# Set-up of a one-core LSTM kernel in another order: load order over two queues, searches before low halves, three PSUM banks for three sums

## The reference

```python
xW = jnp.einsum('ntd,dg->ntg', x, Wx) + b          # x (16, 512, 512), Wx (512, 2048)
def step(carry, xw_t):
    prev_h, prev_c = carry
    a = xw_t + prev_h @ Wh                          # Wh (512, 2048)
    i = jax.nn.sigmoid(a[:, :Hdim])
    f = jax.nn.sigmoid(a[:, Hdim:2 * Hdim])
    o = jax.nn.sigmoid(a[:, 2 * Hdim:3 * Hdim])
    g = jnp.tanh(a[:, 3 * Hdim:])
    next_c = f * prev_c + i * g
    next_h = o * jnp.tanh(next_c)
    return ((next_h, next_c), next_h)
# output: x + all hidden states
```

## Time and profile before

| | us |
|---|---|
| median of 3 runs | 2008.93 (2007.4 to 2013.11) |
| the profiled execution's own time | 2012.29 |
| its span, first to last instruction | 2010.5 |
| VectorE busy in it | 1843.2 |
| TensorE busy in it | 1919.7 |

### The profile page before, as it was taken

The page is one execution under the profiler, slowest core; times in us unless marked ns, Lnnn a source line. Parts: engine busy times, 40 slices in busy tenths (PEclk is TensorE's granted clock), DMA queues, the critical chain, the costliest instruction groups (busy, mean ns, idle before and its releaser), DMA issues.

```text
span 2010.5 us, 144062 instructions
## 1 busy us (share of the span) xinstructions
PE 1919.7 (95%) x65620; PEld 1625.9 (81%) x65620; DVE 1843.2 (92%) x9227; ACT 926.2 (46%) x3217; POOL 2.4 (0%) x13
## 2 busy tenths in 40 slices
PE   0799999999999999999999999999999999999998
PEld 0688888888888888888888888888888888888887
DVE  6899999999999999999999999999999999999998
ACT  2444444444444444444444444444444444444444
POOL 0000000000000000000000000000000000000000
PEclk9999999999999999999999999999999999999999
DMA  4000000000000000000000000000000000000000
GB/s 194 9 20 25 22 14 26 26 21 25 16 19 26 20 26 25 10 25 25 20 25 26 10 25 26 20 26 26 10 25 26 21 25 16 19 26 26 21 15 15
DMA packets 15876, 51.46 MB, mean 26 GB/s; under 512 B 1824, under 2 KB 1824, under 8 KB 14240
## 3 DMA queue, kind: packets, MB, share of 16 engines
q1 hardware_dynamic: 14400, 37.76, 5.3%
q10 hardware_dynamic: 864, 4.49, 0.5%
HBM read 25.46 MB, written 16.78 MB: 21 GB/s over the span
## 4 chain that ended last, share of the span: by engine, by line
PE 72%; DVE 23%; issue 2%; ACT 2%; DMA 1%; SPq 0%; ACTq 0%; DVEq 0%
PE acc L235 34%; PE acc L241 20%; PE acc L247 17%; DVE turned L411 5%; DVE preact L415 4%; DVE products L419 2%; DVE h_halves L442 2%; DVE o_gate L423 2%; DVE h_halves L433 2%; DVE h_feat L437 1%; DVE gates L427 1%; DVE out_ring L465 1%; DMA wx<-in_wx 1%; ACT x_halves L176 1%; DVE w_tops L301 1%
## 5 line engine op out<-in xcount | busy, mean ns | idle before, releaser
L235 PE MATMUL acc<-wx_high,x_halves 128*32 128x256 f16 x16384 | 936.6, 273 | 15.8 <-ACT acc L190 9.3
L235 PE MATMUL acc<-wx_low,x_halves 128*32 128x256 f16 x16384 | 935.8, 273 | 2.7 <-issue 2.4
L241 PE MATMUL acc<-wh_low,h_halves 128*32 128x256 f16 x16384 | 723.5, 274 | 23.9 <-DVE wh_low L315 6.2
L247 PE MATMUL acc<-wh_high,h_halves 128*32 128x256 f16 x16384 | 723.0, 274 | 0.3 <-issue 0.3
L204 ACT ACTIVATE gates<-preact 128x128 f32<-128x128 f32 x1024 | 318.5, 311 | 794.6 <-DVE preact L415 794.6
L411 DVE STREAM_TRANSPOSE turned<-acc 128x256 f32<-128x256 f32 x1024 | 457.1, 446 | 71.0 <-PE acc L247 68.9
L241 PEld LDWEIGHTS acc<-wh_low,h_halves 128*32 128x32 f16 x16384 | 388.2, 96 | 165.3 <-DVE h_halves L433 137.1
L235 PEld LDWEIGHTS acc<-wx_high,x_halves 128*32 128x32 f16 x16384 | 457.7, 97 | 36.8 <-ACT acc L190 11.7
L235 PEld LDWEIGHTS acc<-wx_low,x_halves 128*32 128x32 f16 x16384 | 458.8, 97 | 15.5 <-issue 6.3
L247 PEld LDWEIGHTS acc<-wh_high,h_halves 128*32 128x32 f16 x16384 | 360.9, 96 | 111.8 <-issue 1.1
L190 ACT ACTIVATE acc<-b_rows 128x256 f32<-128x256 f32 x1024 | 345.9, 369 | 0.8 <-issue 0.3
(11 more groups left out here) (57 smaller groups left out, 183.8 us busy)
## 6 DMA issues: line engine op xcount, KB each, us to landing
x_ring<-in_x SPq DMA_DIRECT2D x32, 512.0 KB, 4.3
out<-out_ring SPq DMA_DIRECT2D x64, 256.0 KB, 2.3
wx<-in_wx SPq DMA_DIRECT2D x4, 1024.0 KB, 13.4
wh<-in_wh ACTq DMA_DIRECT2D x4, 1024.0 KB, 17.9
b_rows<-in_b ACTq DMA_DIRECT2D x1, 256.0 KB, 4.5
h_feat<-in_h ACTq DMA_DIRECT2D x1, 32.0 KB, 6.8
```

The lines of the kernel that those rows point to most:

```text
L235: pe.matmul(acc[par][n][32 * j:32 * j + 32, 0:GL], x_halves[:, slot, c], w[:, c, n * Q + j], start=False, stop=False, skip_group_check=True)
L241: pe.matmul(acc[par][n][32 * j:32 * j + 32, 0:GL], h_halves[1 - par][:, c, 0:2], w_low["wh"][:, c, n * Q + j], start=False, stop=False, sk ...
L247: last = pe.matmul(acc[par][n][32 * j:32 * j + 32, 0:GL], h_halves[1 - par][:, c, 1:3], w_high["wh"][:, c, n * Q + j], start=False, stop=c ...
```

## The change

The loop is the same. In the set-up:

- Every chunk of a weight matrix is loaded in two halves of 0.5 MB (4 KB a partition), one on each queue; both halves count on the chunk's semaphore, and the search waits for 32 and not 16. SP's order is Wx halves, x, Wh halves, x; ACT's is Wx halves, h0, Wh halves, bias. Each queue issues 10 DMAs in the set-up, where it issued 6.
- VectorE searches all of Wx, then x, h0 and all of Wh, and only then writes low halves; the bias comes after them.
- ScalarE writes the high halves of x between the high halves of Wh.
- The three sums lie in three PSUM banks (`wx_sums`, `wh_sums`, `x_sums`), and TensorE sums Wx first, then x.

```diff
         @block.sync
         def _(sp):
+            for c in range(C):
+                sp.dma_start(w32["wx"][:, c, 0:Q], wx[:, c, 0:Q]).then_inc(w_loaded["wx"][c], 16)
             sp.dma_start(x_ring[0][:], x[:, 0:CHUNK, :]).then_inc(x_loaded[0], 16)
             for c in range(C):
-                sp.dma_start(w32["wx"][:, c], wx[:, c]).then_inc(w_loaded["wx"][c], 16)
+                sp.dma_start(w32["wh"][:, c, 0:Q], wh[:, c, 0:Q]).then_inc(w_loaded["wh"][c], 16)
...
         @block.scalar
         def _(act):
+            for c in range(C):
+                act.dma_start(w32["wx"][:, c, Q:], wx[:, c, Q:]).then_inc(w_loaded["wx"][c], 16)
+            act.dma_start(h0_feat[:], h0).then_inc(h0_loaded, 16)
+            for c in range(C):
+                act.dma_start(w32["wh"][:, c, Q:], wh[:, c, Q:]).then_inc(w_loaded["wh"][c], 16)
             act.dma_start(b_rows[:], bias).then_inc(b_loaded, 16)
-            act.dma_start(h0_feat[:], h0).then_inc(h0_loaded, 16)
-            for c in range(C):
-                act.dma_start(w32["wh"][:, c], wh[:, c]).then_inc(w_loaded["wh"][c], 16)
...
-            act.wait_ge(wh_scale_ready, 1)
-            for c in range(C):
-                high_of_w("wh", 1, c, wh_high_done)
...
+            act.wait_ge(wh_scale_ready, 1)
+            high_of_w("wh", 1, 0, wh_high_done)
             act.wait_ge(x_loaded[0], 16)
             act.wait_ge(x_scale_ready, 1)
             high_of_x(0, 0)
+            high_of_w("wh", 1, 1, wh_high_done)
             high_of_x(0, 1)
+            high_of_w("wh", 1, 2, wh_high_done)
+            high_of_w("wh", 1, 3, wh_high_done)
...
         @block.tensor
         def _(pe):
             pe.wait_ge(ones_ready, 1)
+            pe.wait_ge(tops_ready, 1)
+            pe.matmul(wx_sums[:, 0:1], ones[:], tops[:, 0:1], start=True, stop=True).then_inc(sums_ready, 1)
             pe.wait_ge(x_top_ready, 1)
...
             for c in range(C):
                 search_w("wx", 0, c)
             dve.wait_ge(dve_setup, count[0])
             dve.tensor_reduce(tops[:, 0:1], w_tops[:, 0], AX.X, ALU.max).then_inc(tops_ready, 1)
-            search_w("wh", 1, 0)
+            dve.wait_ge(x_loaded[0], 16)
+            dve.tensor_reduce(x_top[:], x_ring[0][:], AX.XY, ALU.max, apply_absolute_value=True).then_inc(x_top_ready, 1)
             dve.wait_ge(sums_ready, 1)
...
-            for c in range(1, C):
+            for c in range(C):
                 search_w("wh", 1, c)
-                low_of_w("wx", 0, c - 1, wx_high_done, wx_low_done)
...
-            low_of_x(0, 0)
-            low_of_x(0, 1)
             for c in range(C):
                 low_of_w("wh", 1, c, wh_high_done, wh_low_done)
+                if c < 2:
+                    low_of_x(0, c)
```

More of the change, by code:

```diff
@@ L84, in lstm_kernel @@
         acc = [[psum(f"acc{p}{n}", [128, 512], F32) for n in range(NG)] for p in range(2)]
-        sums = psum("sums", [128, 512], F32)
+        wx_sums = psum("wx_sums", [128, 512], F32)
+        wh_sums = psum("wh_sums", [128, 512], F32)
+        x_sums = psum("x_sums", [128, 512], F32)
         w_loaded = {k: [sem(f"{k}_loaded{c}") for c in range(C)] for k in ("wx", "wh")}
@@ L156, in _ @@
         def _(act):
-            act.dma_start(b_rows[:], bias).then_inc(b_loaded, 16)
+            for c in range(C):
+                act.dma_start(w32["wx"][:, c, Q:], wx[:, c, Q:]).then_inc(w_loaded["wx"][c], 16)
             act.dma_start(h0_feat[:], h0).then_inc(h0_loaded, 16)
             for c in range(C):
-                act.dma_start(w32["wh"][:, c], wh[:, c]).then_inc(w_loaded["wh"][c], 16)
+                act.dma_start(w32["wh"][:, c, Q:], wh[:, c, Q:]).then_inc(w_loaded["wh"][c], 16)
+            act.dma_start(b_rows[:], bias).then_inc(b_loaded, 16)
             def high_of_w(k, n, c, done):
@@ L223, in _ @@
             pe.wait_ge(ones_ready, 1)
+            pe.wait_ge(tops_ready, 1)
+            pe.matmul(wx_sums[:, 0:1], ones[:], tops[:, 0:1], start=True, stop=True).then_inc(sums_ready, 1)
             pe.wait_ge(x_top_ready, 1)
-            pe.matmul(sums[:, 8:9], ones[:], x_top[:], start=True, stop=True).then_inc(x_sum_ready, 1)
-            pe.wait_ge(tops_ready, 1)
-            pe.matmul(sums[:, 0:1], ones[:], tops[:, 0:1], start=True, stop=True).then_inc(sums_ready, 1)
+            pe.matmul(x_sums[:, 0:1], ones[:], x_top[:], start=True, stop=True).then_inc(x_sum_ready, 1)
             pe.wait_ge(tops_ready, 2)
-            pe.matmul(sums[:, 1:3], ones[:], tops[:, 1:3], start=True, stop=True).then_inc(sums_ready, 1)
+            pe.matmul(wh_sums[:, 1:3], ones[:], tops[:, 1:3], start=True, stop=True).then_inc(sums_ready, 1)
             def input_part(slot, par, n):
@@ L328, in _ @@
             dve.tensor_reduce(tops[:, 0:1], w_tops[:, 0], AX.X, ALU.max).then_inc(tops_ready, 1)
-            search_w("wh", 1, 0)
+            dve.wait_ge(x_loaded[0], 16)
+            dve.tensor_reduce(x_top[:], x_ring[0][:], AX.XY, ALU.max, apply_absolute_value=True).then_inc(x_top_ready, 1)
             dve.wait_ge(sums_ready, 1)
-            scale_of(0, 1)
+            scale_of(wx_sums, 0, 1)
             dve.tensor_scalar(half_scale[:, 0:1], wx_scale, 0.5, None, ALU.mult).then_inc(wx_scale_ready, 1)
+            dve.wait_ge(h0_loaded, 16)
+            then(dve.tensor_reduce(tops[:, 2:3], h0_feat[:], AX.XY, ALU.max, apply_absolute_value=True))
             dve.wait_ge(wx_scale_ready, 1)
-            for c in range(1, C):
+            for c in range(C):
                 search_w("wh", 1, c)
-                low_of_w("wx", 0, c - 1, wx_high_done, wx_low_done)
             dve.wait_ge(dve_setup, count[0])
             dve.tensor_reduce(tops[:, 1:2], w_tops[:, 1], AX.X, ALU.max).then_inc(tops_ready, 1)
[L339 to L348, removed]
             def x_bound_of():
-                dve.tensor_scalar(x_bound[:], sums[:, 8:9], TINY, None, ALU.max).then_inc(scale_step, 1)
+                dve.tensor_scalar(x_bound[:], x_sums[:, 0:1], TINY, None, ALU.max).then_inc(scale_step, 1)
             def x_exponent_of():
@@ L376, in _ @@
             x_scale_of()
+            low_of_w("wx", 0, 0, wx_high_done, wx_low_done)
+            dve.wait_ge(sums_ready, 2)
+            scale_of(wh_sums, 1, 3)
+            dve.tensor_scalar(half_scale[:, 1:2], wh_scale, 0.5, None, ALU.mult).then_inc(wh_scale_ready, 1)
+            low_of_w("wx", 0, 1, wx_high_done, wx_low_done)
+            dve.tensor_scalar(top_scale[:], wh_scale, 2.0 ** 13, None, ALU.mult)
+            dve.tensor_scalar(h0_cap[:], wh_scale, h0_scale, None, ALU.mult)
+            dve.tensor_copy(factors[:, 0:1], wx_inverse)
+            dve.tensor_scalar(factors[:, 1:2], wh_inverse, 0.5, None, ALU.mult)
+            dve.tensor_copy(factors[:, 2:3], wh_inverse)
+            then(dve.memset(factors[:, 3:4], 1.0))
             dve.wait_ge(scale_step, 3)
@@ L383, in _ @@
             inverses_of(0)
+            low_of_w("wx", 0, 2, wx_high_done, wx_low_done)
+            low_of_w("wx", 0, 3, wx_high_done, wx_low_done)
+            dve.wait_ge(zeroed, 6)
             dve.wait_ge(x_scale_ready, 1)
@@ L389, in _ @@
                                      ALU.mult, ALU.subtract).then_inc(h_ready, NG)
+            dve.wait_ge(b_loaded, 16)
+            dve.tensor_scalar(b_rows[:, :, 64:GL], b_rows[:, :, 64:GL], 0.5, None, ALU.mult).then_inc(b_ready, 1)
             def low_of_x(chunk, q):
```

11 lines of the change are left out of this document (2 added, 9 removed).

## The result

The changed kernel takes 1995.93 us in the median of 4 runs (1994.72 to 1997.31), the kernel before 2008.45 us (4 runs, 2007.40 to 2013.11). The ratio is 0.9931 with a 95% interval of 0.9918 to 0.9945: faster by 0.7%, or 12.5 us between the medians. The profiled execution took 1997.31 us, with a span of 1995.5 us.

What follows compares the result with a forecast made beforehand. VectorE's work and waits set the first step's start: 64.56 − 20.3 + 5.9 + 3 × 0.18 = 50.7 us. The 13.8 us gain off the 2008.9 us median gives 1995.1 us; 8 in 10 range 1991 to 2002.

Steps and rivals of the forecast that it cites:

- What bounds the kernel: Set-up: VectorE decides when the first step starts; its four waits are 20.3 of 64.56 us, the rest its own work.
- The loads: Set-up loads: stream stays at 424 GB/s; Wx's chunks land at 5.9, 8.4, 10.8 and 13.3 us, Wh's last at 24.6.
- 0.9 us from moving to landing: Set-up loads: time added between a chunk's bytes being moved and its landing; bounds 0.7 to 1.2 us.
- tie at Wh's last chunk: VectorE's fourth Wh search would start at 24.6 us, just when its chunk lands; a later load delays everything one for one.
- Two of the signs: Profile after: no VectorE idle time over 0.3 us after the first search; Wh searches back to back from 18.0 to 26.9.
- holes in the stream: Rival, set-up loads: short transfers leave holes costing 7.2 us; start at 57.9 us, time 2002.3 us; chance 0.08.
- the two queues did not hinder each other: Rival, slower: two queues reading halves of one row hinder each other; at 205 GB/s the time is 2015 us; chance 0.02.
- The walk: VectorE's set-up followed instruction by instruction: Wx searched by 15.6 us, Wh by 26.9, last low halves at 50.8.
- The sum: Set-up: VectorE's work unchanged, only idle time shrinks; first step at 50.7 us, gain 13.8 us.
- Size of transfers: Rule against the forecast, set-up loads: at 341 GB/s the start would move 5.1 us and the time be 2000.2 us.
- The clock: First step at half speed after 4.0 us idle; rivals: clock stays high, 1993.2 us, or rises later, 1997.0; chance 0.08 each.
- x's order: ScalarE in set-up: x's high halves stood behind four chunks of Wh, making VectorE wait 6.2 us; that wait goes.

Runs made afterwards that it cites:

- the versions in which GpSimd stretched VectorE's work: Changed kernel with GpSimd writing low halves of one chunk each of Wx and Wh, or of Wx only: ratio 0.9954 and 0.9922 to the kernel before.

## Why the prediction was right

**What bounds the kernel.** That the start of the first step is all that moves, and that it is VectorE's work plus its idle time, held: 43.25 us of work in 50.92 us. The exceptions are the versions in which GpSimd stretched VectorE's work, and, by 0.2 us, the one with low halves between the searches, in which TensorE's x product ended last.

**The loads.** Chunks every 2.47 us from 5.9 us on were predicted, and they came at 5.48, 8.40, 10.93 and 13.47. The first was 0.4 us early, so 0.9 us from moving to landing was too much for it. The last two gaps of 2.53 and 2.54 us are what 414 GB/s make of 1.049 MB, where 424 was assumed; the first gap of 2.92 is mostly the early first chunk. 5.48 + 1.13 + 0.27 = 6.9 us of idle time stand against 6.4 predicted; VectorE's work came out 0.2 us less, and the first step is 0.2 us behind the 50.7 us of the sum. The predicted tie at Wh's last chunk was there, and it cost 0.27 us. Two of the signs in the prediction did not come true in size: VectorE idled 0.63 us ahead of the second search, where nothing over 0.3 was to be seen, and it did wait for a chunk of Wh, by those 0.27 us. There were no holes in the stream, and the two queues did not hinder each other: the DMA share was 1.03 from 8 to 24 us, and one queue with the same halves gave 411 GB/s.

**The walk.** Predicted and measured: end of the last search of Wh 26.9 and 27.4, Wh's scale for ScalarE 30.8 and 31.15, ScalarE done 42.0 and 42.15, its slack ahead of Wh's last low halves 6 and 6.2, first x product 43.2 and 43.35 (for the bias from ScalarE, not only for x's low halves, which ended at 43.30), first step 50.8 and 50.92.

**The sum.** 13.8 us were predicted; the first step moved by 13.64 and the medians by 12.5. The difference between the two last numbers is well inside the scatter of the loop, 12.9 us between two profiles of one kernel. That the median came within 0.9 us of the forecast of 1995.1 is for that reason partly luck; the start of the first step is what bears the mechanism out.

**Size of transfers.** The 341 GB/s that the Trainium skill gives ("DMA: Bandwidth & Descriptors", section "Bandwidth") would have put the start at 55.8 us, an estimate from that figure. Queued one behind the other, transfers of 0.5 MB gave 411 to 414 GB/s and those of 1 MB 419 to 424, so the measurement decides against the size of that cost here; its direction is right, and it is worth 0.6 us.

**The clock.** The prediction said the idle stretch (4.0 us, measured 3.97) would leave the first step at half speed, and it did. It also said the profile would show this as 0.50 in the clock's column. That was wrong; the column stayed at 1.00, and only the matmuls per microsecond show it. The same holds for a reading that the prediction took from the earlier trace rows: beside the first x product the column says 1.00, but the product ran at half speed (64 matmuls in 3.54 us), so its 3.5 us are a time at half speed. Where the first step follows it at once, the step's matmuls are at full speed (0.62 us for 16, with x's order alone), so the clock rises about where the product ends, and the column has no mark of that. The length of the slow start was not fixed either: first step to second tanh is 7.55 to 8.39 us in the eight profiles in which TensorE idled 3.9 us or more ahead of the first step.

**The parts.** The prediction credited the loads (14.1 us of waits) and x's order (6.2 us) and nothing else. Less the 6.4 us that it left standing, that is 7.7 us for the loads. Undone or done alone, the new loads gave 8.7 us and x's order 6.3 us. The two add to 1.4 us more than 13.64. The kernel with the loads of before starts its first step that much later than the one with x's order alone (59.65 and 58.22 us), and the rows suggest why: in it x's and h0's searches and the bias stand behind Wx and no longer fill the time before Wx lands. No run varied that by itself. The banks, the second queue and the searches of both matrices ahead of the low halves gave nothing. The bias's later place was not tried alone.

## What to carry to other kernels

In a set-up that one engine's work bounds, add up its idle time and what each piece waits for: the gain of a new order is that sum less what it leaves, and nothing was gained here by an order that only shuffles the work (low halves between the searches or behind them). When two operands share one saturated load stream, load first the one that is needed first; neither a second queue nor smaller pieces gave bandwidth here. Look also at what a stall does behind it: a TensorE that idled 4 us before a serial loop began it at half speed, and 60 throwaway matmuls took back 1.7 us.

## What the runs showed of the hardware that was not expected

- The granted clock's record can read 1.00 while TensorE runs at half speed: 77 matmuls in 4.03 us, then 145 in 3.78 us, both with 1.00 beside them. Counting matmuls per microsecond shows the speed.
- An elementwise GpSimd instruction of some 4 us can hold a VectorE instruction of 0.17 us until it ends (1.62 and 4.10 us), while VectorE's reduces beside it keep their 2.29 us.
- Two executions of the same program differed by 12.9 us in a loop of 1942 us. 6.7 us of it are short waits of TensorE for nothing that the profile shows; the rest is open. The steps over 3.86 us were 42 in one and 82 in the other.
- Transfers of 0.5 MB with 4 KB rows ran at 411 to 414 GB/s, those of 1 MB with 8 KB rows at 419 to 424, on one queue as on two.
